# Another order for the first stage of an attention, MLP and FFN layer: step durations, hand-over gaps and leads of the planner replaced

## The chip, the cores and the metric

One Trainium2 chip, one core. The metric is the device time of one execution in microseconds (us), the median of the runs shown.

## The reference, cut to what matters

The layer works on 2 batches of 512 rows of 1024 channels. First comes a block with causal self-attention and a small gated MLP, each wrapped in a "read" and a "write" of a residual of 256 x 4 channels; then a gated feed-forward block whose three weights are a base plus a scaled sign.

```python
qkv_in = rat_read(hidden, attn_read_w, ..., 3)        # 1024 -> 3 x 256, each normalised
attn   = attention(qkv_in, qkv_w, pos)                # 16 heads of 16, rope, causal softmax
hidden = rat_write(hidden, attn, ...)                 # softplus, exp, gated update of the residual
g, u   = split(rat_read(hidden, mlp_read_w, ..., 2))
mlp    = silu(g @ ctx_w[0].T) * (u @ ctx_w[1].T)      # 256 -> 1024
hidden = rat_write(hidden, mlp, ...)
# feed-forward, 1024 -> 3584 -> 1024; each weight w of w1, w3, w2:
w      = base + mean(abs(w - base)) * sign(w - base)
out    = hidden + (silu(norm(hidden) @ w1.T) * (norm(hidden) @ w3.T)) @ w2.T
```

## The kernel before, in words

The kernel has two stages. The **second stage** is the feed-forward block: 28 slices of 128 inner channels in 14 groups of two. Products run as three fp32r passes of high and low parts: `gate` (L969, operands `xnT` and `w_hi`/`w_lo`, into PSUM) and the product with `w2` (L1068). Its order is written out by hand in each engine's loop and isn't touched.

The **first stage** is everything before it. It has 1061 steps, each a few instructions of one engine, named (stage, tile or unit, part); below I write them as `finish6.0`. The stages are:

- `front` t (8 tiles of 128 rows): layer norm, turn (L824), read product (L843), statistics, `qkv` product (L858), rope, turn into `big`.
- `fill`, `use`, `weigh`: attention in 16 groups (batch, half of the queries, quad of heads). `fill` puts scores into the four banks `quad` (L905 and L908 for the row maxima, L915 and L920 for the turned scores); `use` is the maximum on DVE (L1372) or the exponential on ACT (L1122); `weigh` is the product with the values (L878). The `quad` banks are filled one unit after another: `fill` u+1 waits for `use` u. `turnmax` turns the maxima and lowers the queries by them, `out` copies the weighed values, `row` divides by the sums.
- `back` t: the residual write after attention and the read before the MLP. `mlp` (4 blocks of 256 rows, 8 steps each): product on PE (L1022), `Silu` on ACT (L1250, into `sgate`), product on DVE (L1525, into `inner`).
- `finish` t: the write after the MLP. Part 0 is its product on PE (L952, which waits for all 8 `inner` of its block), parts 1 to 8 softplus and factors (on DVE L1416 to L1434), part 9 on POOL adds the reloaded x to `wr_q` (L1619), part 12 is SP's reload of x into `qk_xa`, parts 13 and 10 on POOL add into `hid` (L1670, L1624), part 11 on DVE are two products over 128x768 (L1438, L1441), parts 14 to 16 the statistics (last instruction L1309).
- `norm` t: scaling into `works` on ACT (L1193), turn on PE (L824), high part on ACT (L1202), low part on DVE (`xnT_lo`, L1557). `early`: the first 12 pieces of the second stage's `gate` products, for batch 0.
- `measure` n (84 weight slices): load of weight and base (SP), their difference (DVE L1547, every third on POOL L1675), sum of magnitudes on ACT (L1268). `coef` sums them up. `raw` and `prep` load the first three slices again and make weights of them: difference on POOL (L1633), sign on ACT, `coeff` times sign plus base on DVE (L1448), high part on ACT, low part on DVE (L1458).

**What sets the order.** `phase_one_order` is a list scheduler that runs when the kernel is built. Each step has an engine and a cost from `WORK` (a third number is the part for which DVE shares SBUF access with POOL), `before` lists what it depends on, and of the ready steps the one with the smallest rank is put next into its engine's program:

```python
rank = start - PULL * weight[key] - lead(key)
```

`weight` is the cost of the longest chain behind the step, for measurements `MEASURE_WEIGHT` times how many are left, and `lead` comes from the tables `FIRST` (by stage and stretch) and `AHEAD` (by part). Each engine then runs its steps strictly in this order. PSUM banks for the steps in `HOLD` and the work set of a tile are chosen in the same pass. ACT changes its table of functions when an `mlp` step follows another kind or the reverse (L1250, L1252). At the end of the stage every engine goes on with its own loop of the second stage.

## Time and profile before

| | |
|---|---|
| median of 3 runs | 1403.0 us |
| the three runs | 1399.58, 1403.0, 1406.03 us |
| profiled execution, its own time | 1408.62 us |
| its span (first to last instruction) | 1406.8 us |
| mean granted TensorE clock | 0.958 |
| busy: PE, DVE, ACT, POOL | 1292.9, 868.6, 530.1, 361.9 us |
| ACT table loads in the MLP steps (L1250, L1252) | 6 and 6 |

The profiled execution is one run. Its time lies 5.6 us above the median of the three runs, and 1.8 us above its own span. The page's strip of 40 slices (35.2 us each) has PE at 9 tenths from slice 15 on; the second stage begins at 492.65 us. Busy time of PE is no measure of its peak, since its matmuls overlap.

### The profile page before, as it was taken

What the parts mean: (1) busy time and instruction counts of PE and PEld (TensorE: products, weight loads), DVE (VectorE), ACT (ScalarE), POOL (GpSimd) and SP (SyncE); (2) the same over time, 40 slices, a digit from 0 to 9 for tenths busy, and PEclk for the clock granted to TensorE, in tenths of its full rate; (3) what the DMA queues carried; (4) which work ended last, traced back from release to release, by engine and by line L of the source; (5) the groups of instructions that cost most, each with busy time, mean ns of one, the idle gap of its engine ahead of it and who ended that gap; (6) DMA issues with size and microseconds to landing.
All of it is one profiled execution on the core that took longest, in us unless ns stands there. A gap on an engine that the chain in (4) does not pass through costs nothing.

```text
span 1406.8 us, 16747 instructions
## 1 busy us (share of the span) xinstructions
PE 1292.9 (92%) x6548; PEld 1015.8 (72%) x6548; DVE 868.6 (62%) x1135; ACT 530.1 (38%) x809; POOL 361.9 (26%) x197
## 2 busy tenths in 40 slices
PE   4887788877887899999999999999999999999998
PEld 4754555545665678888888888888788888888887
DVE  6768777778878865546564546363645546554544
ACT  4776665855655432222222222222222222222220
POOL 2222333233234422222222222222222222222210
PEclk9998988987899899999999999999999999999999
DMA  8476887577731222322222222232222232222312
GB/s 339 147 273 252 287 285 267 208 288 274 268 132 31 105 90 93 105 102 90 90 94 97 109 90 90 90 106 102 91 90 90 95 111 94 90 90 90 116 34 120
DMA packets 53826, 197.55 MB, mean 140 GB/s; under 512 B 6626, under 2 KB 6900, under 8 KB 53236
## 3 DMA queue, kind: packets, MB, share of 16 engines
q1 hardware_dynamic: 53748, 196.49, 38.7%
q8 instruction: 52, 0.85, 0.2%
q14 instruction: 26, 0.21, 0.0%
HBM read 192.27 MB, written 4.19 MB: 140 GB/s over the span
## 4 chain that ended last, share of the span: by engine, by line
PE 72%; DVE 15%; issue 5%; ACT 5%; DMA 2%; POOL 1%; SPq 0%; DVEq 0%; ACTq 0%
PE pair L969 42%; PE quad L1068 17%; PE pair L952 2%; DVE negwide L1372 2%; PE quad L915 1%; DMA ctxw<-in_mean_w 1%; DVE raw_w L1448 1%; DVE hid L1438 1%; PE pair L1022 1%; PE quad L905 1%; PE pair L843 1%; ACT prob L1122 1%; PE pair L824 1%; DVE wr_q L1425 1%; DVE big L1547 1%
## 5 line engine op out<-in xcount | busy, mean ns | idle before, releaser
L1633 POOL TENSOR_TENSOR raw_w<-raw_w,raw_base 128x1024 f32<-128x1024 f32 x84 | 215.5, 2567 | 661.5 <-DMA raw_base<-in_mean_w 661.5
L969 PE MATMUL pair<-xnT_hi,w_hi 128*128 128x512 f32 x880 | 343.8, 391 | 3.3 <-DVE xnT_lo L1557 3.3
L969 PE MATMUL pair<-xnT_lo,w_hi 128*128 128x512 f32 x880 | 343.6, 390 | 0.0
L969 PE MATMUL pair<-xnT_hi,w_lo 128*128 128x512 f32 x880 | 343.5, 390 | 0.0
L1590 DVE TENSOR_TENSOR hf<-sgf,pair 128x512 f32<-128x512 f32 x56 | 38.5, 688 | 282.1 <-PE pair L969 282.1
L1182 ACT ACTIVATE w_hi<-raw_w 128x1024 fp32r<-128x1024 f32 x84 | 88.8, 1058 | 324.0 <-DVE raw_w L1448 323.8
L969 PEld LDWEIGHTS pair<-xnT_hi,w_hi 128*128 128x128 f32 x880 | 166.1, 189 | 38.6 <-issue 2.7
L969 PEld LDWEIGHTS pair<-xnT_lo,w_hi 128*128 128x128 f32 x880 | 165.9, 189 | 34.5
L969 PEld LDWEIGHTS pair<-xnT_hi,w_lo 128*128 128x128 f32 x880 | 165.9, 189 | 34.4
L1068 PE MATMUL quad<-w_hi,h_hi 128*128 128x512 f32 x448 | 175.4, 391 | 9.3 <-DVE hid L1570 9.3
L1448 DVE SCALAR_TENSOR_TENSOR raw_w<-raw_w,coeff,raw_base 128x1024 f32<-128x1024 f32 x84 | 166.8, 1988 | 19.9 <-ACT raw_w L1165 19.9
L1068 PE MATMUL quad<-w_lo,h_hi 128*128 128x512 f32 x448 | 174.4, 389 | 0.0
L1068 PE MATMUL quad<-w_hi,h_lo 128*128 128x512 f32 x448 | 174.3, 389 | 0.0
L1570 DVE TENSOR_TENSOR hid<-hid,quad 128x512 f32<-128x512 f32 x208 | 138.1, 683 | 56.5 <-PE quad L1068 56.5
L1458 DVE TENSOR_TENSOR w_lo<-raw_w,w_hi 128x1024 fp32r<-128x1024 f32 x84 | 106.0, 1264 | 34.2 <-ACT w_hi L1182 34.2
L1286 ACT ACTIVATE h_hi<-hf 128x512 fp32r<-128x512 f32 x56 | 35.4, 632 | 230.9 <-DVE hf L1590 230.9
L1068 PEld LDWEIGHTS quad<-w_hi,h_hi 128*128 128x128 f32 x448 | 84.1, 188 | 31.0 <-issue 14.0
L1068 PEld LDWEIGHTS quad<-w_lo,h_hi 128*128 128x128 f32 x448 | 84.1, 188 | 17.7
L1068 PEld LDWEIGHTS quad<-w_hi,h_lo 128*128 128x128 f32 x448 | 84.1, 188 | 17.0
L1165 ACT ACTIVATE raw_w<-raw_w 128x1024 f32<-128x1024 f32 x84 | 87.9, 1047 | 0.0
L1281 ACT ACTIVATE sgf<-pair 128x512 f32<-128x512 f32 x54 | 32.1, 595 | 108.2 <-PE pair L969 108.1
L1595 DVE TENSOR_TENSOR h_lo<-hf,h_hi 128x512 fp32r<-128x512 f32 x56 | 51.8, 924 | 19.6 <-ACT h_hi L1286 19.6
(234 smaller groups left out, 1561.4 us busy)
## 6 DMA issues: line engine op xcount, KB each, us to landing
raw_w<-in_w SPq DMA_DIRECT2D x84, 512.0 KB, 3.8
raw_base<-in_mean_w SPq DMA_DIRECT2D x84, 512.0 KB, 4.6
part<-in_w SPq DMA_DIRECT2D x28, 512.0 KB, 4.1
part<-in_mean_w SPq DMA_DIRECT2D x28, 512.0 KB, 5.3
ctxw<-in_w SPq DMA_DIRECT2D x28, 512.0 KB, 4.8
ctxw<-in_mean_w SPq DMA_DIRECT2D x28, 512.0 KB, 6.3
big<-in_w SPq DMA_DIRECT2D x20, 512.0 KB, 3.8
big<-in_mean_w SPq DMA_DIRECT2D x20, 512.0 KB, 4.8
```

Source lines behind the costliest of these rows:

```text
L969: a = pe.matmul(banks[gate_bank(u, b)], ww[:, k, :], xx[:, k, :], start=k == 0 and n == 0, stop=k == KF - 1 and n == 2)
L1068: a = pe.matmul(banks[m % 4], hh[:, t * P:(t + 1) * P], ww[:, half * BANK:(half + 1) * BANK], start=kk == 0 and n == 0, stop=kk == GROUP - ...
L1165: act.activation(w[:, :], w[:, :], ACT.Sign).then_inc(f_sign, 1)
L1182: act.activation(hi, raws[n % RAWS][0][:, :], ACT.Copy).then_inc(f_hi, 1)
L1281: act.activation(sgf[b][:, :], banks[gate_bank(4 * g + s, b)], ACT.Silu).then_inc(g_silu, 1)
L1286: act.activation(ht[j % GROUP][0][:, b * SEQ:(b + 1) * SEQ], hf[b][:, :], ACT.Copy).then_inc(g_hhi, 1)
L1448: dve.scalar_tensor_tensor(w[:, :], w[:, :], coeff[:, k:k + 1], base[:, :], ALU.mult, ALU.add).then_inc(f_w, 1)
L1458: dve.tensor_tensor(lo, raws[n % RAWS][0][:, :], hi.bitcast(F32), ALU.subtract).then_inc(f_lo, 1)
L1570: dve.tensor_tensor(target, rows, banks[m % 4].rearrange("p (c k j) -> p c k j", c=2, j=32), ALU.add).then_inc(o_acc, 1)
L1590: dve.tensor_tensor(hf[b][:, :], sgf[b][:, :], banks[gate_bank(u, b)], ALU.mult).then_inc(g_mul, 1)
L1595: dve.tensor_tensor(ht[j % GROUP][1][:, cols], hf[b][:, :], ht[j % GROUP][0][:, cols].bitcast(F32), ALU.subtract).then_inc(g_hlo, 1)
L1633: pool.tensor_tensor(w[:, :], w[:, :], base[:, :], ALU.subtract).then_inc(f_diff, 1)
```

## The change

No instruction is added or taken out by hand, and the dependencies in `before` stay as they are. What changes are the numbers that the list scheduler works with, and two lines of its clock:

- the costs in `WORK` and `found_work`, most of them a little lower than before (exponentials, copies), the weighing and masks a little higher;
- `HOP`, the gap between a step and one that waits for it, 0.05 in place of 0.12;
- a new table `AHEAD_OF`: an engine counts as free 0.16 (PE), 0.08 (DVE), 0.09 (ACT) or 0.04 us (POOL) before its step's end;
- `MEASURE_WEIGHT`, `PULL` and all of `FIRST` and `AHEAD`.

The diff, cut to its core (line numbers of the changed kernel are 2 higher from the first stage's programs on, 3 within the scheduler):

```diff
-RAT = [("PE", 1.35), ("DVE", 0.3), ("PE", 0.25), ("ACT", 0.3), ("PE", 0.5), ("ACT", 1.7), ("DVE", 1.85, 0.2),
-       ("ACT", 0.87), ("DVE", 2.5, 0.25), ("POOL", 1.85), ("POOL", 0.75), ("DVE", 2.05, 2.05)]
+RAT = [("PE", 1.48), ("DVE", 0.27), ("PE", 0.27), ("ACT", 0.26), ("PE", 0.59), ("ACT", 1.48), ("DVE", 1.52, 0.2),
+       ("ACT", 0.83), ("DVE", 2.68, 0.25), ("POOL", 1.81), ("POOL", 0.72), ("DVE", 1.94, 1.94)]
...
-LANDING, HOP, TABLE = 2.5, 0.12, 1.3
+LANDING, HOP, TABLE = 2.5, 0.05, 1.3
+
+AHEAD_OF = {"PE": 0.16, "DVE": 0.08, "ACT": 0.09, "POOL": 0.04, "SP": 0.0}
...
-            return "PE", 0.1 + 0.53 * cols / 256
+            return "PE", 0.22 + cols / 600
...
-        free_at[engine] = start + us
+        free_at[engine] = start + us - AHEAD_OF[engine]
...
-MEASURE_WEIGHT, PULL = 4.89, 0.00247
+MEASURE_WEIGHT, PULL = 5.161, 0.00237
```

Three places where the order comes out otherwise are shown here.

**The last MLP block, DVE.** These are the steps `mlp24.2` to `mlp31.2` (`inner`), between the end of `finish5.8` and the products of the residual (`hid` with `wr_a` and `wr_q`, `finish4.11` and `finish5.11`). Before:

```order
L1525 TENSOR_TENSOR inner<-pair,sgate 128x256 x2
L1525 TENSOR_TENSOR inner<-quad,sgate 128x256
L1438 TENSOR_TENSOR hid<-hid,wr_a 128x3x8x32
L1441 TENSOR_TENSOR hid<-hid,wr_q 128x3x8x32
L1525 TENSOR_TENSOR inner<-pair,sgate 128x256
L1438 TENSOR_TENSOR hid<-hid,wr_a 128x3x8x32
L1441 TENSOR_TENSOR hid<-hid,wr_q 128x3x8x32
L1525 TENSOR_TENSOR inner<-quad,sgate 128x256
```

Now:

```order
L1527 TENSOR_TENSOR inner<-quad,sgate 128x256
L1527 TENSOR_TENSOR inner<-pair,sgate 128x256 x4
L1527 TENSOR_TENSOR inner<-quad,sgate 128x256 x3
L1440 TENSOR_TENSOR hid<-hid,wr_a 128x3x8x32
L1443 TENSOR_TENSOR hid<-hid,wr_q 128x3x8x32
```

All eight MLP products now stand ahead of the four large residual products. On POOL, the three differences of the second stage's first weights (`raw_w`) stood behind all of that tile pair's work before:

```order
L1619 TENSOR_TENSOR wr_q<-wr_q,qk_xa 128x768 x2
L1670 TENSOR_TENSOR hid<-hid,qk_xa 128x8x32
L1624 TENSOR_TENSOR hid<-hid,wr_s 128x8x32 x2
L1633 TENSOR_TENSOR raw_w<-raw_w,raw_base 128x1024 x3
```

Now they stand around `finish4.9`, right behind the last difference of a measurement (`late`):

```order
L1677 TENSOR_TENSOR late<-late 128x1024
L1635 TENSOR_TENSOR raw_w<-raw_w,raw_base 128x1024
L1621 TENSOR_TENSOR wr_q<-wr_q,qk_xa 128x768
L1635 TENSOR_TENSOR raw_w<-raw_w,raw_base 128x1024 x2
L1672 TENSOR_TENSOR hid<-hid,qk_xa 128x8x32
L1626 TENSOR_TENSOR hid<-hid,wr_s 128x8x32
L1621 TENSOR_TENSOR wr_q<-wr_q,qk_xa 128x768
```

So `finish4.13` (L1672), behind which SP reloads x for tile 5, stands behind all three of them.

**The attention's second group, PE.** `weigh1` (L878) and the scores of `fill2` (L905, L908), both ready after the first exponential. Before:

```order
L824 MATMUL pair<-ident,wideqk 128x128 x8
L858 MATMUL pair<-wqkv,yT 128x256 x6
L878 MATMUL pair<-prob,vaug 32x256 x4
L878 MATMUL pair<-prob,vaug 32x128 x4
L905 MATMUL quad<-big 128x128 x4
L908 MATMUL quad<-maskb,identb 128x128 x4
```

Now:

```order
L826 MATMUL pair<-ident,wideqk 128x128 x8
L860 MATMUL pair<-wqkv,yT 128x256 x6
L907 MATMUL quad<-big 128x128 x4
L910 MATMUL quad<-maskb,identb 128x128 x4
L907 MATMUL quad<-big 128x256 x4
L910 MATMUL quad<-maskb,identb 128x128 x4
L880 MATMUL pair<-prob,vaug 32x256 x4
L880 MATMUL pair<-prob,vaug 32x128 x4
```

The next scores stand ahead of the weighing. Over the whole stage eight `weigh` steps move behind a `fill` that stood behind them (1, 3, 5, 18, 20, 22, 29, 38) and three the other way (7, 14, 27). `fill4` had `front3.15`, `front4.13` and `weigh3` between itself and `fill3`; now `front4.11` and `front5.6` stand there.

**The first MLP block, ACT.** Before, its eight `Silu` steps (`sgate`) came in three pieces, with a table load at each end of each:

```order
L1250 ACT_TABLE_LOAD
L1250 ACTIVATE sgate<-pair 128x256
L1268 ACTIVATE big,absum<-big 128x1024
L1250 ACTIVATE sgate<-pair 128x256
L1252 ACT_TABLE_LOAD
L1152 ACTIVATE wr_a<-pair 128x256
```

Now it is one piece:

```order
L1252 ACT_TABLE_LOAD
L1252 ACTIVATE sgate<-pair 128x256 x2
L1270 ACTIVATE big,absum<-big 128x1024
L1252 ACTIVATE sgate<-pair 128x256
L1270 ACTIVATE part,absum<-part 128x1024
L1252 ACTIVATE sgate<-pair 128x256 x2
```

Four table loads less here; the third MLP block, one piece before, is in two now (`back6.18` and `finish3.7` stand between `mlp20.1` and `mlp21.1`), two loads more. The whole program has 13 table loads in place of 15. The same ordering moves the measurements back: ahead of the last exponential (`use47`) ACT had 65 of them and has 61 now, and `raw0.0` to `raw2.0` are issued by SP behind all measurements, where they stood among them before.

## Rows read from the trace of the kernel before

**Rows 1.** Windows: busy time (x instructions) of each engine, clock, DMA, by stretch

```profile
core 0: us, PE busy (x) PEld busy (x) DVE busy (x) ACT busy (x) POOL busy (x), PEclk, DMA share, GB/s
...
404.00:420.00 16.00, 14.89 (x43) 7.95 (x42) 9.98 (x28) 7.30 (x16) 4.17 (x7) 0.86 0.00 1
...
433.60:443.00 9.40, 2.49 (x23) 2.33 (x21) 9.33 (x8) 4.39 (x6) 7.14 (x3) 0.80 0.06 21
...
492.65:1406.80 914.15, 901.11 (x3960) 742.43 (x3960) 489.38 (x498) 227.15 (x274) 199.99 (x78) 1.00 0.27 95
```

**Rows 2.** Timeline of PE: start us, us, what, idle before and its releaser

```profile
442.94 2.87 PE L952 MATMUL pair<-wcat,inner 128*128 128x376 f32 x4 [6.91 <-DVE inner L1525]
```

**Rows 3.** Timeline of DVE, last MLP block

```profile
428.63 0.42 DVE L1525 TENSOR_TENSOR inner<-quad,sgate 128x256 f32<-128x256 f32 x1
...
429.56 0.42 DVE L1525 TENSOR_TENSOR inner<-pair,sgate 128x256 f32<-128x256 f32 x1 [0.30 <-ACT sgate L1250]
...
433.64 1.88 DVE L1438 TENSOR_TENSOR hid<-hid,wr_a 128x768 f32<-128x768 f32 x1
435.55 2.98 DVE L1441 TENSOR_TENSOR hid<-hid,wr_q 128x768 f32<-128x768 f32 x1
...
438.79 2.76 DVE L1438 TENSOR_TENSOR hid<-hid,wr_a 128x768 f32<-128x768 f32 x1
...
442.46 0.42 DVE L1525 TENSOR_TENSOR inner<-quad,sgate 128x256 f32<-128x256 f32 x1
```

**Rows 4.** Timeline of POOL; last its line L1633, ns min/median/max

```profile
421.97 1.82 POOL L1619 TENSOR_TENSOR wr_q<-wr_q,qk_xa 128x768 f32<-128x768 f32 x1 [6.15 <-issue]
...
432.35 8.39 POOL L1633 TENSOR_TENSOR raw_w<-raw_w,raw_base 128x1024 f32<-128x1024 f32 x3
...
L1633 POOL TENSOR_TENSOR raw_w<-raw_w,raw_base x6: 2351/2396/3055, 432.4 to 487.9; 128x1024 f32<-128x1024 f32 x6
```

**Rows 5.** Timeline of DVE: steps with two SBUF operands, and a wait for PE

```profile
424.06 0.19 DVE L1417 SCALAR_TENSOR_TENSOR wr_z<-wr_b,wr_a 128x48 f32<-128x48 f32 x1
...
449.80 0.28 DVE L1412 TENSOR_TENSOR wr_b<-pair,bias_ab 128x120 f32<-128x120 f32 x1 [1.41 <-PE pair L952]
...
462.36 1.72 DVE L1309 SCALAR_TENSOR_TENSOR x_stat<-x_stat 128x1 f32<-128x1 f32 x1
...
471.17 2.54 DVE L1438 TENSOR_TENSOR hid<-hid,wr_a 128x768 f32<-128x768 f32 x1
```

**Rows 6.** Timeline of DVE, end of the first stage

```profile
478.92 0.95 DVE L1438 TENSOR_TENSOR hid<-hid,wr_a 128x768 f32<-128x768 f32 x1
...
482.46 0.15 DVE L1305 TENSOR_SCALAR x_stat<-x_stat 128x1 f32<-128x1 f32 x1
...
483.28 2.33 DVE L1309 SCALAR_TENSOR_TENSOR x_stat<-x_stat 128x1 f32<-128x1 f32 x1 [0.60 <-POOL x_stat L1628]
...
491.37 1.23 DVE L1557 TENSOR_TENSOR xnT_lo<-quad,xnT_hi 128x1024 fp32r<-128x1024 f32 x1 [2.31 <-ACT xnT_hi L1202]
```

**Rows 7.** Timeline of ACT, first MLP block

```profile
250.38 1.28 ACT L1252 ACT_TABLE_LOAD   x1
251.67 0.38 ACT L1152 ACTIVATE wr_a<-pair 128x256 f32<-128x256 f32 x1
```

**Rows 8.** Timeline of ACT: last exponential, last measurement; then DVE's line L1547

```profile
321.07 1.45 ACT L1122 ACTIVATE prob<-quad 128x1536 f32<-128x1536 f32 x1 [2.41 <-PE quad L920]
...
403.72 1.06 ACT L1268 ACTIVATE late<-late 128x1024 f32<-128x1024 f32 x1 [0.93 <-POOL late L1675]
...
L1547 DVE TENSOR_TENSOR part<-part x28: 1207/1217/2264, 48.7 to 395.0; 128x1024 f32<-128x1024 f32 x28
```

**Rows 9.** Timelines of PE and ACT, second and third attention group

```profile
65.91 0.86 PE L878 MATMUL pair<-prob,vaug 128*32 128x256 f32 x16
...
80.63 0.50 PE L905 MATMUL quad<-big 32*128 32x128 f32 x8
...
75.48 1.45 ACT L1122 ACTIVATE prob<-quad 128x1536 f32<-128x1536 f32 x1 [0.23 <-PE quad L920]
```

More of the change, by code:

```diff
@@ L129 @@
+    "mlp": [("PE", 1.89), ("ACT", 0.38), ("DVE", 0.42)],
+    "finish": [("PE", 5.32)] + RAT[1:8] + [("DVE", 3.55, 1.25)] + RAT[9:] + [("SP", 2.0), ("POOL", 0.73), ("DVE", 1.71),
+                                                                           ("POOL", 0.55), ("DVE", 0.16, 0.16)],
+    "measure": [("SP", 3.5), ("POOL", 2.35), ("ACT", 1.25)],
     "x": [("SP", 2.0)],
     "ctx": [("SP", 7.0)],
-    "diag": [("DVE", 4.0, 4.0)],
-    "raw": [("SP", 2.0), ("POOL", 2.4), ("ACT", 1.06)],
-    "coef": [("DVE", 0.35), ("PE", 0.35), ("DVE", 0.2)],
@@ L134 @@
-    "prep": [("DVE", 1.3, 1.3), ("ACT", 1.08), ("DVE", 1.25, 1.25)],
-    "norm": [("ACT", 1.25), ("PE", 1.1), ("ACT", 1.05), ("DVE", 1.25)],
-    "early": [("PE", 1.4)] * 4,
+    "diag": [("DVE", 3.84, 3.84)],
+    "raw": [("SP", 2.0), ("POOL", 2.35), ("ACT", 1.05)],
+    "coef": [("DVE", 0.2), ("PE", 0.3), ("DVE", 0.15)],
+    "prep": [("DVE", 1.28, 1.28), ("ACT", 1.05), ("DVE", 1.22, 1.22)],
+    "norm": [("ACT", 1.24), ("PE", 1.04), ("ACT", 1.01), ("DVE", 1.21)],
+    "early": [("PE", 1.53)] * 4,
@@ new lines @@
+FIRST = {"back": (-2.4, -2.4, -2.8, -2.9), "coef": (-1.7, -2.1), "ctx": (8.5,), "diag": (32.4, 31.3), "early": (-10.5,),
+         "fill": (14.8, 1.5, -0.9, 1.2), "finish": (-0.6, -1.3, -3.7, -10.9), "front": (-4.2, -4.1, -4.5, -5.7),
+         "measure": (0.1,), "mlp": (0.8, -0.7, -0.2, -4.1), "norm": (2.8, 1.9, -3.8, -2.8),
+         "out": (-5.2, -5.7, -1.4, -5.4), "prep": (2.9,), "raw": (-3.5,), "row": (0.3, -1.1, -0.7, 2.9),
+         "turnmax": (3.2, 2.9, 1.7, 0.1), "use": (-1.6, -1.5, 8.2, -1.9), "weigh": (4.2, 1.5, 0.5, 0.4), "x": (6.1,)}
@@ new lines @@
+AHEAD = {"back": (2.8, 9.4, 8.6, 3.7, 3, 4.4, 3, 1.8, 2.1, 1.7, 5.4, 2.7, 2.2, 2.5, 0.6, 6.6, 3.6, 3, 2.7, 2, 2.6),
+         "coef": (-5.9, 3, -7.1), "ctx": (-2.3,), "diag": (-30.7,), "early": (0.4, -7.6, -2.3, -2.7), "fill": (0.1,),
+         "finish": (1.4, 3, 5.6, 3.7, 6.4, 0.6, 1.5, 0.2, 0.3, 2.7, -0.1, 2.3, 2.7, -4, -0.1, 4.4, -1.2),
+         "front": (5.2, 4.6, 5.5, 5, 14.4, 5.8, 48.1, 5.4, 5.4, 7.6, 7.5, 5.4, 4.7, 21.2, 5.8, 5.2, 5.8),
+         "measure": (3.6, 0.1, -0), "mlp": (-1.8, 0.3, 8.3), "norm": (-2.5, -11.4, 1, 9.3), "out": (5.1,),
+         "prep": (-4.3, -5.8, -8.7), "raw": (1, 0.3, -2.8), "row": (12.4, 0.9, 0.4, 4.5), "turnmax": (-0.8, 9.8),
+         "use": (2.1,), "weigh": (-1,), "x": (2.8,)}
```

38 lines of the change are left out of this document (11 added, 27 removed).

## The prediction

> **What bounds the kernel now.** I read the windows by stretch first. From 492.65 us on the second stage keeps PE busy for 901.11 of 914.15 us at full granted clock [rows 1]. Its instructions and their order stay as they are, so those 914 us stay, and the change can only move the moment at which they begin. Ahead of it no engine is full over the whole stage; what ends last changes from place to place, so I looked for the end first.
>
> PE's timeline shows the largest hole: `finish6.0` starts at 442.94 after 6.91 us idle, released by DVE's `inner` [rows 2]. DVE's timeline tells why. The eight MLP products of the last block begin at 428.63, 0.93 us apart [rows 3], but after six of them the four large products of `finish4.11` and `finish5.11` stand in the queue, mixed with the last two. And these are slow: 1.88, 2.98 and 2.76 us [rows 3], where the same instruction takes 0.95 [rows 6]. POOL's timeline shows the other side: three `raw_w` differences fill 432.35 to 440.74 [rows 4], 2.80 us each in place of the 2.40 of their median. The two engines took turns. The last `inner` ends at 442.88.
>
> From there DVE sets the pace to the end: in the windows it is busy 9.33 of 9.40 us [rows 1], and its last full statistics step ends at 482.61 [rows 6]. Then a chain of small steps follows: the final `x_stat` took 2.33 us in place of 0.15, beside the second stage's first POOL difference, and the last `xnT_lo` runs from 491.37 [rows 6]. It ends the stage.
>
> **The change, part by part.** The sum is made against the profiled execution, 1408.62 us; the median of the runs shown lies 5.6 us lower, and I shift by that at the end.
>
> (a) The last MLP block. All eight products now go first. Undisturbed, the last would end 7 x 0.93 + 0.42 = 6.9 us after the first begins, at 435.6, and `finish6.0` would start 7.3 us sooner. Against that stands POOL: `raw1.1` and `raw2.1` now follow `finish4.9`, which ended at 423.79 [rows 4], and so meet `finish5.6` and `finish5.8` on DVE. Their small products of two SBUF operands, such as the one at 424.06 [rows 5], wait while a difference runs. The nearest row is the same kind of step behind `finish6.8`, 1.72 us in place of 0.15 [rows 5, 6]; at 424.06 the wait is for a difference that has just begun, about 2.1 us, and for the next one about 0.8. Bounds: 0 (POOL early or late) and two whole differences, 4.8. I take 2.9. Then the last `inner` ends at 438.5, 4.4 us sooner.
>
> The Trainium skill, SBUF — State Buffer, section "SBUF: two separate sides", says that GpSimd and a VectorE operation with two SBUF inputs take one port pair as an exclusive lock, and that whichever starts first holds it for its whole instruction. By that rule the differences cost DVE as much beside `finish5.8` as beside `finish4.11`, which speaks against this move; the rival "lock" below is that case.
>
> DVE still has the four large products to do, 4 x 0.96 = 3.9 us, which before were done by 442.88. At 438.5 it is 4.4 us ahead in time and 3.9 us behind in work, so 0.5 is won there. Behind that, the rows show 1.41 us of waiting for `finish6.0`, 1.72 - 0.15 = 1.57 on the step at 462.36 and 2.54 - 0.95 = 1.59 on the product at 471.17 (`finish6.11` against `finish7.9`) [rows 5], 4.6 in all. I expect 2.6 to be left, since `finish6.0` ends earlier than it is needed and `finish7.8` (mostly PSUM operands) now stands between. Together DVE's last full statistics step comes 2.5 us sooner.
>
> (b) The very end. Before, 10.0 us pass from 482.61 to 492.65. In it the last turn of `norm7` waited on PE behind two `early` pieces. Now `early2.3` stands ahead of `norm7.1`, and `norm6.3` ahead of the last `x_stat`; the `early` pieces themselves begin sooner, since `norm3.3` and `prep` are through some 10 us earlier. What can't be shortened is the wait for POOL and the blocked step (0.6 + 2.33) and the last DVE step (1.23) [rows 6]; ACT, PE and ACT stand between, so I keep 8.0. Gain 2.0, between 0 and 3.5.
>
> (a) and (b) give 4.5, between 2 lost and 9 won.
>
> (c) Measurements. Four of them (61 to 64) leave the time ahead of the last exponential at 321.07 [rows 8]: three differences on DVE, 3 x 1.22 = 3.7 us [rows 8], and four magnitudes on ACT. They reappear where DVE has room: 404 to 420 is busy 9.98 of 16 us [rows 1]. Gain between 0 and 3.7; I take 3.0, as DVE is the fuller of the two.
>
> (d) Attention. In five places net (eight less three) the scores no longer wait for `weigh`, 0.86 us each [rows 9]: 4.3 at most. At one place more is moved: `fill4` began at 80.63 although its exponential had ended at 76.93 [rows 9]; two shorter steps (2.8 us) now stand there. But every other chain of the stage has to keep up, and tiles 4 to 7 of `front` are pushed back for it. Between 0 and 6; I take 2.0.
>
> (e) Tables. Four loads less in the first MLP block, 4 x 1.28 = 5.1 us of ACT [rows 7]; two more in the third block, 2.6 us, which I count at nothing, since ACT is the least busy of the three engines that hand on there (38% of the span); uncovered they would cost 2.6. In the first block ACT has gaps too, so a quarter counts: 1.3, between -2.6 and 5.1. The row shows the next activation start 0.01 us after a load's end [rows 7]. The Trainium skill, ScalarE: Activation LUTs, section "What ACT_TABLE_LOAD costs", counts about 1.38 us of drain on top, 2.66 for a switch; by that the term would be twice as large and the sum 1.4 us lower. The trace doesn't agree.
>
> The loads behind the measurements (`raw0.0` to `raw2.0`) and the later reload of x for tile 5 cost nothing as long as their cover holds: `raw2.1` ends near 429, the reload lands 4 to 5 us later, `finish5.9` is through near 436, and DVE wants it at about 444.
>
> Sum: 4.5 + 3.0 + 2.0 + 1.3 = 10.8. 1408.6 - 10.8 = 1397.8 in the profile, and **1392.2** for the median.
>
> **The rivals.**
> *Only the end moves.* (c) to (e) come to nothing, since they free an engine that others don't wait for. For it: no engine is full before 428 us, and the planner has put other work in each gap. Then -4.5, for the median 1398.5. That is no change by my measure; what a measurement of this kernel can tell from none is about 0.5%, 7 us.
> *Lock.* Every `raw_w` difference blocks one of DVE's small products for its whole 2.40 us: 3 x 2.40 = 7.2 in place of 2.9. The term (a) is gone, the rest stays: -10.8 + 4.3 = -6.5, 1396.5. It decides if POOL has its three differences ready just when `finish4.8` to `finish5.8` run.
> *The measurements come too late* (slower). After the last exponential 23 are left in place of 19. Before, the 19 took from 321 to 404.8 [rows 8], 4.4 us each; at that pace the last ends near 422. On POOL the last difference and `raw0.1`, whose load SP now issues behind all measurements, stand ahead of `finish4.9`, `finish4.13` and so of the reload for tile 5. That chain has about 8 us in hand (436 against 444), `prep0.0` more. So it decides from a last measurement at 430 on, 4.75 us each. At 5.5 it ends at 447, 17 us too late, one to one: -10.8 + 17 = +6 to +7, 1409.5. The slot that each load waits for is freed by ACT, so a slower ACT or DVE in the MLP blocks would do it.
>
> **How the numbers follow.** Forecast case 0.56, only the end 0.22, lock 0.09, too late 0.13. The forecast case's own range is 1382 to 1396 (its terms at their bounds don't all come together). The 8-in-10 range takes in the two small cases and half of the slow one: 1381 to 1405. Faster by over 0.5% (below 1396): 0.57, the forecast case and a little of the next. Within: 0.30. Slower: 0.13.
>
> **What would show it.** PE's hole in front of `finish6.0` (L954 after) shrinks from 6.9 us to under 4; the eight `inner` come in one run 0.93 apart; `finish4.11` and `finish5.11` take 0.95 to 1.0 each, and the waits turn up in L1419 and L1426. The last magnitude on ACT ends near 420 rather than 404.8. The last exponential comes 3 to 8 us sooner than 321, and the windows show 914 us from the first full batch-1 gate on, beginning near 482. It is wrong if the last exponential isn't earlier, if PE waits longer ahead of the last MLP block, or if DVE shows a wait for `coeff`. If the second stage itself changes by more than 2 us, my first sentence is wrong.

## The result, and the profile after

Beside 4 runs of the kernel before with a median of 1401.8 us, 4 runs of the changed kernel gave 1412.5 to 1428.9, median 1425.5: ratio 1.0148, 95% interval 1.0080 to 1.0217. It is slower by some 20 us; I had forecast 10.8 faster. The kernel before ran 104 times more beside the experiments, mean 1404.6 us, standard deviation 3.7; the changed one has 8 runs in all, mean 1422.6 (6.6), a loss of 18.0. Below I compare means. One execution, the profiled one of `middle_after`, took 2142.9 us at a granted clock of 0.556 and stands in no mean.

| | before | after |
|---|---|---|
| profiled execution, its span | 1408.6, 1406.8 us | 1428.9, 1427.1 us |
| mean granted clock of it | 0.958 | 0.949 |
| `fill38` begins, `use38` begins | 263.12, 269.65 | 268.42, 285.54 |
| `fill39` begins | 271.58 | 289.22 |
| last exponential, last magnitude | 321.07, 403.72 | 337.83, 439.78 |
| `finish6.0` begins | 442.94 | 460.64 |
| second stage begins, its length | 492.65, 914.15 | 511.46, 915.64 |

A step's start is that of its first instruction; `use38` is the exponential of `fill38`'s scores. The windows of the changed kernel, columns as in [rows 1] (this one was opened 0.06 us ahead of the first product), have the second stage nearly unchanged, and it begins 18.8 us later:

```profile
511.40:1427.10 915.70, 902.48 (x3960) 743.38 (x3960) 487.49 (x499) 227.17 (x275) 202.97 (x78) 1.00 0.27 95
```

Of these 18.8 us, 16.8 are there at the last exponential, and 17.6 already at `fill39`. PE's timeline of the changed kernel shows how they come about:

```profile
268.42 1.15 PE L917 MATMUL quad<-big 32*128 32x256 f32 x16 [0.20 <-DVE big L1383]
269.50 12.35 PE L1024 MATMUL pair<-inT,ctxw 128*128 128x256 f32 x56
282.78 5.32 PE L954 MATMUL pair<-wcat,inner 128*128 128x376 f32 x16 [0.93 <-DVE inner L1527]
...
289.22 0.71 PE L907 MATMUL quad<-big 32*128 32x512 f32 x3
```

At 268.42 `fill38` puts its scores into the `quad` banks. Then come the seven other products of the first MLP block (L1024) and `finish0.0` (L954, 5.32 us), and only 20.8 us later `fill39`; before, that distance was 8.5 us. ACT's timeline of the same place:

```profile
267.69 1.28 ACT L1252 ACT_TABLE_LOAD   x1
268.99 0.38 ACT L1252 ACTIVATE sgate<-pair 128x256 f32<-128x256 f32 x1
...
281.89 0.38 ACT L1252 ACTIVATE sgate<-pair 128x256 f32<-128x256 f32 x1
282.29 1.28 ACT L1254 ACT_TABLE_LOAD   x1
283.58 1.02 ACT L1233 ACTIVATE yn<-pair,stat_back 128x256 f32<-128x256 f32 x2
...
285.54 1.87 ACT L1124 ACTIVATE prob<-quad 128x2048 f32<-128x2048 f32 x1
```

The scores of `fill38` were ready at 269.57. But the exponential stands behind the whole block: eight `Silu` (L1252) that come at PE's pace, mostly 1.7 us apart, the table load back, `back2.18` and a magnitude. It begins at 285.54, 16.0 us after its scores; before, it was 5.4.

What I had looked at was right in its form. The last MLP block on DVE, to compare with [rows 3], and DVE's small steps ahead of it, with [rows 5]:

```profile
445.01 1.43 DVE L1419 SCALAR_TENSOR_TENSOR wr_z<-wr_b,wr_a 128x48 f32<-128x48 f32 x1
...
449.26 1.80 DVE L1426 TENSOR_TENSOR wr_r<-wr_r,wr_b 128x48 f32<-128x48 f32 x1
...
453.63 0.42 DVE L1527 TENSOR_TENSOR inner<-quad,sgate 128x256 f32<-128x256 f32 x1
...
460.17 0.42 DVE L1527 TENSOR_TENSOR inner<-quad,sgate 128x256 f32<-128x256 f32 x1 [0.51 <-ACT sgate L1252]
460.51 0.95 DVE L1440 TENSOR_TENSOR hid<-hid,wr_a 128x768 f32<-128x768 f32 x1
461.49 0.96 DVE L1443 TENSOR_TENSOR hid<-hid,wr_q 128x768 f32<-128x768 f32 x1
```

The eight `inner` come in one run 0.93 us apart, the large products take 0.95 and 0.96, the waits turned up in L1419 (1.43 in place of 0.19), L1424 (1.39) and L1426 (1.80), and `finish6.0` follows without a hole. The hole has gone to the front: the first `inner` comes 115.8 us after the last exponential, not 107.6. ACT's last exponential and last magnitude, which answer to [rows 8]:

```profile
337.83 1.45 ACT L1124 ACTIVATE prob<-quad 128x1536 f32<-128x1536 f32 x1 [1.61 <-PE quad L922]
...
439.78 1.04 ACT L1270 ACTIVATE late<-late 128x1024 f32<-128x1024 f32 x1
```

PE's timeline at the end of the first stage:

```profile
508.00 1.09 PE L826 MATMUL quad<-ident,work 128*128 128x128 f32 x8 [1.79 <-ACT work L1195]
511.46 0.79 PE L971 MATMUL pair<-xnT_hi,w_hi 128*128 128x512 f32 x1 [2.37 <-DVE xnT_lo L1559]
...
512.91 0.63 PE L971 MATMUL pair<-xnT_hi,w_hi 128*128 128x512 f32 x1
```

A product of that stage takes 0.79 and 0.63 us here and 0.39 later: PE had waited 1.79 and 2.37 us, and from 512 to 514 us the windows show its granted clock at 0.50, the lower of its two levels.

### The profile page after: what moved, and what is told of

It is laid out like the page before. It is cut to its first block, busy times and chain, and to the rows that moved or that the text cites. A ratio compares the mean times of both kernels' runs of the same rounds, so it can differ in the third digit from the quotient of the medians.

```text
span 1427.1 us, 16746 instructions
## 1 busy us (share of the span) xinstructions
PE 1303.3 (91%) x6548; PEld 1022.1 (72%) x6548; DVE 877.4 (61%) x1135; ACT 525.0 (37%) x807; POOL 367.9 (26%) x197
## 4 chain that ended last, share of the span: by engine, by line
PE 73%; DVE 17%; issue 5%; ACT 4%; POOL 0%; DMA 0%; SPq 0%; DVEq 0%; ACTq 0%
PE pair L971 41%; PE quad L1070 17%; DVE negwide L1374 2%; PE pair L954 2%; PE quad L917 2%; PE quad L954 2%; PE quad L907 1%; DVE raw_w L1450 1%; DVE ctxw L1549 1%; ACT prob L1124 1%; DVE wr_q L1427 1%; PE pair L860 1%; PE pair L1024 1%; DVE hid L1440 1%; DVE hid L1443 1%
## 5 line engine op out<-in xcount | busy, mean ns | idle before, releaser
L1450 DVE SCALAR_TENSOR_TENSOR raw_w<-raw_w,coeff,raw_base 128x1024 f32<-128x1024 f32 x84 | 159.9, 1905 | 21.9 <-ACT raw_w L1167 21.9
L1460 DVE TENSOR_TENSOR w_lo<-raw_w,w_hi 128x1024 fp32r<-128x1024 f32 x84 | 108.9, 1297 | 35.7 <-ACT w_hi L1184 35.7
```

What stands on the lines that cost most here:

```text
L1450: dve.scalar_tensor_tensor(w[:, :], w[:, :], coeff[:, k:k + 1], base[:, :], ALU.mult, ALU.add).then_inc(f_w, 1)
L1460: dve.tensor_tensor(lo, raws[n % RAWS][0][:, :], hi.bitcast(F32), ALU.subtract).then_inc(f_lo, 1)
```

## The experiments

Every order experiment has one edit to the planner, and above it the names of all 1061 steps in the order wanted. The short diffs further down show what moves in that list, or how it was put together:

```diff
-            rank = start - PULL * weight[key] - lead(key)
+            rank = PLACE[f"{stage}{t}.{part}"]
```

With the sequence of either kernel in it, this gives that kernel's program, whatever the costs. So the numbers of `WORK`, `HOP` and `AHEAD_OF` do nothing but set the order.

### The same kernel again, and the exponential moved ahead

`again` is the changed kernel unaltered.

> The changed kernel once more, unaltered, to see how far its own executions lie apart. Theory 'queue' (the loss comes from the order, above all from the exponential use38 that stands behind the whole first MLP block on ACT): median 1418 to 1428, and fill39 begins at 286 to 292 us in this profile too, use38 10 us or more after its scores are ready. Rival 'clock' (a lower granted TensorE clock in the run profiled made the trace look as it does): a run with a granted clock of 0.957 or more shows fill39 near 275 and a time near 1405.

Measured: mean 1422.0, ratio 1.0109 (1.0048 to 1.0171). Its profiled execution was the fastest of the four, 1414.2 us at a clock of 0.954:

```profile
252.88 1.15 PE L917 MATMUL quad<-big 32*128 32x256 f32 x16 [0.52 <-DVE big L1383]
253.95 12.35 PE L1024 MATMUL pair<-inT,ctxw 128*128 128x256 f32 x56
267.24 5.32 PE L954 MATMUL pair<-wcat,inner 128*128 128x376 f32 x16 [0.93 <-DVE inner L1527]
...
273.68 0.70 PE L907 MATMUL quad<-big 32*128 32x512 f32 x3
```

`fill38` comes at 252.88, 15.5 us sooner than in the other profile of the same program and 10.2 sooner than before; but `fill39` comes 20.8 us after it, as there. So two things must be kept apart: a fixed loss of 12 us behind `fill38`, and a stretch ahead of it whose length differs by 15 us between runs. For the same reason the last exponential of this execution, 8.4 us faster than its kernel's mean, begins at 322.24, only 1.2 us later than in the profile of the kernel before, and its second stage 2.9 us later; places are better compared within a stretch than from the start. Part of either theory holds: the time (1422.0) and the late exponential are those of "queue", but its "fill39 at 286 to 292 again" failed.

`exp_first` puts `fill38`/`use38` ahead of the first MLP step:

```diff
-PE   mlp0.0 fill38.0 mlp1.0 mlp2.0 mlp3.0 ... mlp7.0 finish0.0 finish0.2 finish0.4 fill39.0
+PE   fill38.0 mlp0.0 mlp1.0 mlp2.0 fill39.0 mlp3.0 ... mlp7.0 finish0.0 finish0.2 finish0.4
```

> One edit to the changed kernel: fill38 and use38 stand ahead of the first MLP step, fill39 and use39 behind mlp2; nothing else moves. Theory 'queue': the attention's chain gets back what it lost behind the MLP block, 8 to 12 us of the 17.6 by which fill39 was late, so the time falls to 1411 to 1417 and fill47 begins at 323 to 327 in place of 335.2. Rival 'filled anyway': the attention catches up but the first MLP block, now broken open, makes finish and the last MLP blocks late by as much; fill47 earlier by 8 us and finish6.0 (L954) by under 3, time 1421 or more. Rival 'measurements': they are what is late (60.2 by 35 us); then fill47 gains under 3 us as well.

Measured: mean 1429.2, ratio 1.0161 (1.0107 to 1.0215): nothing gained, 6.6 us above the changed kernel. Its PE:

```profile
255.39 1.22 PE L1010 MATMUL quad<-big 32*128 32x256 f32 x16 [2.26 <-DVE big L1476]
...
263.49 1.14 PE L1000 MATMUL quad<-big 32*128 32x512 f32 x8
...
272.91 3.69 PE L1117 MATMUL pair<-inT,ctxw 128*128 128x256 f32 x16 [1.32 <-DVE inner L1620]
277.54 5.32 PE L1047 MATMUL pair<-wcat,inner 128*128 128x376 f32 x16 [0.93 <-DVE inner L1620]
...
285.51 0.71 PE L1010 MATMUL quad<-big 32*128 32x256 f32 x8
```

`fill39` comes 8.1 us after `fill38`, as wanted, but `fill40` (285.51) then stands behind five more products and `finish0.0`. From `fill38` to `fill47` it takes 74.4 us in place of 66.3. The rival "filled anyway" is right in the time and in its gist, that the work is there and has to be done somewhere. Its picture was another one: it had the attention catch up and `finish` pay, but here the attention itself didn't catch up, since it waits for the same products at `fill40`.

### Where the loss arises: the two orders cut and joined

`head_before`, `head37_before` and `head24_before` take the order of the kernel before up to `weigh47`, `fill37` and `fill24`, and behind it the changed kernel's. `head24_after` is the reverse of the last. (In `head24_before` one pair more, `turnmax8.0` and `weigh24.0`, stands as in the kernel before.)

```diff
+SEQUENCE = before[:before.index("weigh47.0") + 1]
+SEQUENCE += [step for step in after if step not in SEQUENCE]
```

> The order of the kernel before up to the end of the attention (weigh47), then the order of the changed kernel. Theory: the whole loss lies ahead of that cut, and the end of the stage gains what my terms (a) and (b) say: the second stage begins 4.5 us sooner than in the kernel before, time 1395 to 1400 beside 1401.8. Rival 'shift': what stands behind the cut is worth nothing or loses (the trace of the changed kernel has its last full statistics step and its second stage 1.5 us later still than the attention's end explains): 1402 to 1405.

> The order of the kernel before up to fill37, then the changed kernel's order, which finds six MLP products already done. Theory 'deferred MLP': nothing is left of the block to stand in the way of use38; fill38 to fill47 takes 55 to 57 us in place of 66.5, and the time is 1402 to 1408, the end's 3 to 4 us of loss included. Rival 'everything behind fill38 is worse': 62 us or more from fill38 to fill47 and a time of 1411 or more.

> The order of the kernel before up to fill24, then the changed kernel's. If the changed order's own part up to fill24 prepares the low clock that follows, fill24 to fill30 takes 41 to 44 us here as in the kernel before, fill38 comes before 256, and the time is 1408 to 1414, the deferred MLP block and the end still paid. If it is the order behind fill24: fill24 to fill30 takes 46 us or more in part of the runs, and the time is 1417 to 1424.

> The changed kernel's order up to fill24, then the order of the kernel before (which first catches up on 12 measurement steps and 6 others). Theory 'deferred MLP': the loss is made between fill24 and fill47, where the changed order has the first MLP block, 8 products and 8 Silu, in one piece behind fill38: 1400 to 1406. Rival 'low clock early': the changed order's first attention groups leave TensorE at a low clock, 5 to 6 us more of it between fill24 and fill30 in two profiles; then half of the 20 us shows here too, 1409 or more.

| kernel | mean us | ratio to before, 95% | time x (1 - granted clock) | `fill38` at | `fill38` to `fill47` |
|---|---|---|---|---|---|
| before | 1404.6 | | 53.6 | 263.1 | 54.9 |
| `head_before` | 1404.9 | 0.9994 (0.9966 to 1.0022) | 52.8 | 259.1 | 54.9 |
| `head37_before` | 1412.1 | 1.0054 (1.0035 to 1.0073) | 55.9 | 260.9 | 62.9 |
| `head24_before` | 1420.5 | 1.0115 (1.0080 to 1.0150) | 67.8 | 261.6 | 67.5 |
| after (both labels) | 1422.6 | 1.0148 and 1.0109 | 69.7 | 268.4, 252.9 | 66.8, 66.3 |
| `head24_after` | 1416.2 | 1.0085 (1.0064 to 1.0105) | 60.9 | 269.6 | 53.7 |

Read downwards, each step exchanges one piece of the order: the end behind the attention 0.3 us, `fill38` to `weigh47` 7.2, `fill24` to `fill37` 8.4, all that is ahead 2.1. The sum is the 18.0 us; each difference of means is uncertain by 1 to 2.5 us. So the end, on which 4.5 of my 10.8 us rested, is worth nothing as it stands (the rival "shift"), and 15.6 of the 18.0 us lie in the attention's second half. The pieces have these prices only in this direction: `head24_after`, with the changed order up to `fill24` alone, loses 11.6 us and not 2.1. `head37_before` went with its rival (62.9, 1412); `head24_before` with its second case in the time, while `fill24` to `fill30` stayed at 43.8 in the one profile. `head24_after` lost too: it has to catch up on 18 steps left off before `fill24` and takes 53.2 us from there to `fill30` (42.8 before), so its time, which is the one that the rival named, doesn't tell its two theories apart.

What the changed order does is seen from the counts: at `fill24` it has done 12 measurement steps and 6 others fewer than the order before, at `fill38` 19 measurement steps, 17 steps of the first MLP block and 4 of `back` fewer. For that it should be ahead. No gain is seen: the eight profiles with the order before up to `fill37` and no products added have `fill38` at 257.7 to 263.1, mean 260.2; the four with the changed order at 252.9, 255.4, 266.7 and 268.4, mean 260.8. (Four profiles so far apart could hide some us.) The reason that I see, which no run isolates, is that the attention's scores wait for exponentials and these for scores, and that leaving other work off doesn't shorten that chain. The work left off is then paid for behind `fill38`: from there to `fill47` PE is busy 54.3 and 55.5 us in the two profiles of the changed kernel, and 43.6 in the kernel before.

### One step, one block: the converse in the kernel before

`finish_late` moves `finish0` and `finish1` back in the changed kernel, `finish_early` moves `finish0.0` ahead of `fill39` in the kernel before (`back4.12` and `back4.13` fall in behind `fill41` with it), `mlp_late` moves the whole first MLP block behind `fill38` there.

```diff
-PE   mlp6.0 mlp7.0 back2.19 back3.14 fill39.0 ... fill42.0 finish0.0
+PE   mlp6.0 mlp7.0 back2.19 back3.14 finish0.0 fill39.0 ... fill42.0
```

```diff
-PE   ... fill38.0 mlp6.0 mlp7.0 back2.19 back3.14 fill39.0
+PE   ... fill38.0 mlp0.0 mlp1.0 mlp2.0 mlp3.0 mlp4.0 mlp5.0 mlp6.0 mlp7.0 back2.19 back3.14 fill39.0
```

> The changed kernel with the steps of finish0 and finish1 at the progress they have in the kernel before: finish0.0 (5.3 us of PE) stands behind fill44, not ahead of fill39; all else as in the changed kernel. Theory 'finish0 holds the attention' : fill39 begins 5 to 6 us sooner after fill38 (15 in place of 20.8), fill38 to fill47 falls from 66.5 to 58 to 61, and the time by 4 to 8 us, to 1414 to 1419. Rival 'filled anyway': PE has the same products to do before fill47, the segment stays above 64 and the time within 3 us of 1422.

> The converse in the kernel before: finish0.0 alone stands ahead of fill39 (it stood behind fill42). Theory 'finish0 holds the attention': fill39 begins 4 to 6 us later after fill38 (12.5 to 14.5 in place of 8.5) and the whole of it reaches fill47 and the end, 1407 to 1410. Rival 'filled anyway': the product is saved again behind fill42, so that fill38 to fill47 stays within 2 us of 55 and the time within 2 us of 1403.5.

> The kernel before with its first MLP block (mlp0 to mlp7, products, Silu and inner) in one piece behind fill38 and ahead of use38, as the changed kernel has it; nothing else moves. Theory 'deferred MLP': the attention ahead of fill38 gets at most 3 us faster, since its scores wait for exponentials and not for PE, fill39 begins 17 to 21 us after fill38 in place of 8.5, and the time is 1410 to 1415, 6 to 10 us above the kernel before. My term (e), the rival: four table loads less, 1400 to 1404, because fill38 comes as much sooner as use38 is later.

`finish_early`: mean 1411.8, ratio 1.0044 (1.0020 to 1.0069), 7.2 us lost, all but by one step. PE of it:

```profile
260.16 1.15 PE L1010 MATMUL quad<-big 32*128 32x256 f32 x16
261.24 3.72 PE L1117 MATMUL pair<-inT,ctxw 128*128 128x256 f32 x16
...
266.96 5.27 PE L1047 MATMUL pair<-wcat,inner 128*128 128x376 f32 x16
272.17 1.14 PE L1000 MATMUL quad<-big 32*128 32x512 f32 x8
```

`fill39` comes 12.0 us after `fill38` in place of 8.5, and `fill38` to `fill47` takes 61.7 in place of 54.9. The rival is refuted; the theory holds in kind, though `fill39` comes only 3.5 us later and the rest of the 6.8 arises behind it. `mlp_late`: mean 1414.1, ratio 1.0067 (1.0042 to 1.0092), 9.5 us lost. Its PE:

```profile
255.24 1.15 PE L1010 MATMUL quad<-big 32*128 32x256 f32 x16 [0.60 <-DVE big L1476]
256.32 14.08 PE L1117 MATMUL pair<-inT,ctxw 128*128 128x256 f32 x64
...
276.13 1.24 PE L1000 MATMUL quad<-big 32*128 32x512 f32 x4 [3.57 <-ACT prob L1217]
```

and its ACT:

```profile
270.43 0.38 ACT L1345 ACTIVATE sgate<-pair 128x256 f32<-128x256 f32 x1 [1.34 <-PE pair L1117]
270.84 1.28 ACT L1347 ACT_TABLE_LOAD   x1
...
274.23 1.85 ACT L1217 ACTIVATE prob<-quad 128x2048 f32<-128x2048 f32 x1
```

The exponential waits from 256.4 to 274.23 for the block. `fill30` to `fill38` takes 43.0 us, beside 44.4 to 49.2, mean 46.6, in seven profiles with the order before, and `fill38` to `fill47` 9.4 longer. The time is the theory's. This is my term (e) by itself, four table loads less, with the opposite sign. What it doesn't separate is the two queues: the eight products stand ahead of `fill39` on PE as the eight `Silu` stand ahead of `use38` on ACT. `finish_late`: mean 1429.6, ratio 1.0181 (1.0152 to 1.0211). The segment did fall, to 63.2 us, but `fill47` to `mlp8` rose by as much (23.6 in place of 20.4), and from the last exponential to `finish6.0` it took 129.1 us (122.8 and 122.5 in the changed kernel). Neither theory has this: the mean is 7.0 us above the changed kernel, where "filled anyway" allowed 3. So undoing this one move there gains nothing.

### Measurements moved alone

`measures_before` gives the changed kernel the measurement steps, and the load of the MLP weights, at the progress (count of other steps) of the kernel before; `measures_late` the reverse.

```diff
+SEQUENCE = [each measure and ctx step where the other kernel has it, counted in other steps]
```

> The changed kernel with every measurement step and the load of the MLP weights (ctx) at the progress they have in the kernel before, all other steps in the changed kernel's order. Theory 'queue' makes no use of the measurements: under 4 us gained, 1420 to 1426. Rival 'measurements' (with term (c) wrong in sign: measurements and with them the load of the MLP weights come later, and so does the first MLP step): mlp0 begins near 250 in place of 266, and half or more of the 17 us comes back, 1408 to 1417.

> The kernel before with every measurement step and the load of the MLP weights at the progress they have in the changed kernel. My term (c): the differences and magnitudes moved out of the attention give 3 us, 1401 to 1403. Theory 'measurements carry the MLP weights': measure41, behind which that load is issued, comes later, the first MLP block stands in PE's queue and waits for it with the scores behind it; mlp0 begins 5 us or more later than 240 to 244 and the time is 1408 or more. Rival 'neither': within 2 us of 1404.6.

Means 1458.3 and 1449.2, ratios 1.0367 (1.0315 to 1.0419) and 1.0326 (1.0291 to 1.0362): some 36 and 45 us lost, both ways, and from the first attention groups on (`fill11` at 122.4 and 117.2 in place of 110.2 and 111.1). `mlp0` began at 274.8 in the first, not at 250. In `measures_late` the theory of the MLP weights is met to the letter (`mlp0` at 266.4, time over 1408), but `fill11` was late well over 100 us before that load was issued (258.51), so it isn't what these 45 us show; the other theories are off. What the two runs show is that a kind of step can't be exchanged by itself. The price of my term (c) is not measured by them, and stays open.

### The clock: cause, or company?

Over the runs of a kernel time and clock go together: of the 18.0 us between the means, 16.1 are in the column time x (1 - clock). That invites the reading that the order lowers the clock and the clock makes the loss. At one place it can be seen whole, the entry of the second stage. `early_after` puts `early2.3` ahead of `norm7.1` in the kernel before, `tail_early` moves it back in `head_before`, and `warm_entry` adds useless work to `head_before`:

```diff
-PE   norm7.1 early2.3
+PE   early2.3 norm7.1
```

```diff
                 if g == 0:
+                    readers_through(pe, [had_last[gate_bank(0, 1)]])
+                    for k in range(9):
+                        pe.matmul(banks[gate_bank(0, 1)], w13[0][0][:, k % KF, :], xnT[0][0][:, k % KF, :],
+                                  start=True, stop=True)
                     pe.wait_ge(n_lo, TILES)
```

> The converse in the kernel before: early2.3 stands ahead of norm7.1, nothing else moves. Theory 'clock at entry': PE waits 2.4 us ahead of the last gate products, the clock there shows 0.5 to 0.6, and 2 to 4 us are lost, 1404.5 to 1406.5. Rival 'same work, other place': within 1 us of the kernel before; norm7.1 is also delayed by up to 1.4 us, which is a loss without any clock, so that a time 1.4 us longer with products 0.23 apart would be the rival's too.

> The kernel head_before with one step moved: PE's early2.3 (six gate products) stands behind norm7.1 again, as in the kernel before, in place of ahead of it. Theory 'clock at entry': in head_before PE had nothing between norm7.1 (ended 485.1) and the first full batch-1 gate (487.48), its granted clock fell to 0.53, and the first 12 of these products took 0.43 us apart in place of 0.23, 2.4 us; with PE kept busy they run 0.23 apart and the time falls by 2 to 4 us, to 1399 to 1401.5. Rival 'same work, other place': the early products only move, PE waits as long ahead of norm7.1 instead, the clock falls there, and the time stays within 1 us of head_before's 1403.4.

> head_before with nine products more on PE, of no use (batch 0's xnT with the first weights, into the bank that the first batch-1 gate overwrites), ahead of PE's wait for the last xnT_lo; no step moves. Theory 'clock at entry': they fill 2.1 of the 2.4 us that PE waits, the granted clock stays at 1.00, the first 12 gate products come 0.23 us apart in place of 0.43, and a kernel with more work gets 1.5 to 2.5 us faster: 1401 to 1403 beside head_before's mean of 1404.9. Rival 'the clock falls for another reason' (the 1.8 us ahead of norm7.1, or chance): the products are still 0.43 apart, which then delays the gates by up to 1.5 us more: 1405 or more.

`early_after`: mean 1407.0, ratio 1.0017 (0.9999 to 1.0035), 2.4 us lost, which is just about the noise; in its profile the second stage is 1.7 us longer. Its windows, PEclk in the third column from the right:

```profile
486.00:488.00 2.00, 0.87 (x8) 0.63 (x6) 0.04 (x1) 1.08 (x2) 0.25 (x1) 1.00 0.00 0
488.00:490.00 2.00, 0.76 (x3) 0.67 (x4) 1.18 (x1) 1.99 (x3) 0.00 (x0) 0.95 0.00 0
490.00:492.00 2.00, 2.00 (x7) 1.52 (x6) 1.08 (x1) 0.78 (x1) 0.00 (x0) 0.50 0.00 0
492.00:494.00 2.00, 2.00 (x8) 1.58 (x7) 0.80 (x2) 0.00 (x0) 0.00 (x0) 0.70 0.00 0
```

The granted clock goes to 0.50, the level of 1.2 GHz, after PE had waited 2.37 us. `warm_entry`: mean 1402.8, ratio 0.9987 (0.9971 to 1.0003), 2.1 us less than `head_before` (1404.9), standard error 1.3, with nine products more. Its PE:

```profile
482.29 1.09 PE L919 MATMUL quad<-ident,work 128*128 128x128 f32 x8 [1.79 <-ACT work L1292]
483.14 2.34 PE L1142 MATMUL pair<-xnT_hi,w_hi 128*128 128x512 f32 x9
485.76 0.50 PE L1064 MATMUL pair<-xnT_hi,w_hi 128*128 128x512 f32 x1 [0.29 <-DVE xnT_lo L1656]
486.10 0.40 PE L1064 MATMUL pair<-xnT_hi,w_lo 128*128 128x512 f32 x1
```

and its windows:

```profile
484.00:486.00 2.00, 1.71 (x8) 1.10 (x7) 1.23 (x1) 1.97 (x3) 1.62 (x1) 1.00 0.00 0
486.00:488.00 2.00, 2.00 (x10) 1.61 (x10) 0.55 (x1) 1.31 (x2) 0.00 (x0) 1.00 0.00 0
```

The clock stays at 1.00 and the products come 0.23 us apart, where the first 12 in `head_before` came 0.43 apart: 2.4 us in the traces. Here the clock is a cause, of some 2 us; the trace shows it better than the times, which are 1.7 standard errors apart. `tail_early`: mean 1401.7, ratio 0.9984 (0.9967 to 1.0002), 3.2 us under `head_before` (standard error 1.3). In its profile PE waits 3.12 us ahead of `norm7.1` instead, and that turn and `early2.3` are at half clock; the rival named this, but the time fell as the theory had it. Why it did isn't shown.

The rest of the question went to useless transposes (`ident`, 0.13 us each at full clock) in PE's other waits:

```diff
+WARM = {step: (the bank's last user, bank, count), ...}
+                if (stage, t, part) in WARM:
+                    warm(*WARM[stage, t, part])
```

> The changed kernel with transposes of no use on PE (of ident, 0.13 us each at full clock, into a bank whose last reader is done) ahead of six steps before which it waited 1.3 to 2.6 us: fill17, turnmax6, front7.11, turnmax9, fill32, fill36; 56 of them, 7.3 us of PE. No step moves. Theory 'the clock is a cause': the granted clock stays up, less than 64 us are lost to it in place of 69.7, and the time falls to 1413 to 1419. Rival 'the clock goes along': the time stays at 1421 to 1426, the additions at best hidden in the waits; a mean of 1420 or more with an unchanged clock is that case.

> tail_early with such transposes ahead of norm5.1 (22), of norm7.1 (20) and of the wait for the last xnT_lo (11). PE waited there 3.8, 3.1 and about 1 us, and the profile of tail_early shows norm7.1 at 1.97 in place of 1.10 us and ten gate products behind it 0.43 apart. Theory: they run at full clock, the second stage's products begin 2 to 3 us sooner, 1398 to 1400 beside tail_early's mean of 1401.7. Rival 'what ends last is DVE' : the last xnT_lo (483.88) sets the entry and not PE, so at most 1 us: 1400.5 to 1402.

> warm_tail with transposes of no use ahead of nine more steps of the first stage before which PE waited 1.2 to 3.1 us (fill15, front5.15, fill21 left out, fill24, weigh24, fill35, fill47, finish2.0, early0.0). Theory 'the clock is a cause': clock loss below 46 us in place of 50, time 1393 to 1398, faster than all others. Rival 'the clock goes along' or 'fillers get in the way': 1399 to 1404, no better than warm_tail.

| kernel | mean us | ratio to before, 95% | time x (1 - clock) |
|---|---|---|---|
| after | 1422.6 | | 69.7 |
| `warm_gaps` | 1419.4 | 1.0099 (1.0066 to 1.0132) | 55.6 |
| `tail_early` | 1401.7 | 0.9984 (0.9967 to 1.0002) | 49.9 |
| `warm_tail` | 1403.4 | 0.9993 (0.9970 to 1.0015) | 50.3 |
| `warm_all` | 1400.1 | 0.9973 (0.9950 to 0.9996) | 36.9 |

Between 180 and 195 us the changed kernel had run at 0.50 throughout in its first profile and at 0.77 in the second (`again`); in `warm_gaps` it is at 1.00. The window of the changed kernel in its first profile:

```profile
180.00:195.00 15.00, 13.09 (x94) 9.00 (x90) 5.94 (x13) 6.50 (x14) 3.01 (x2) 0.50 0.55 207
```

in `again`:

```profile
180.00:195.00 15.00, 12.23 (x93) 7.66 (x93) 8.68 (x12) 8.62 (x20) 2.35 (x1) 0.77 0.46 152
```

and in `warm_gaps`:

```profile
180.00:195.00 15.00, 11.79 (x129) 8.53 (x124) 10.16 (x15) 8.81 (x19) 3.07 (x3) 1.00 0.73 262
```

14.1 us of lost clock came back, and the time fell by 3.2 (standard error 2.9), which lies between the ranges of the two theories. So a good part of the lost clock lies where PE waits anyway and costs nothing: the 14.1 us were worth hardly more than 9, and most likely 3. (What the added transposes themselves cost isn't separated.) The loss of the changed order is not the 16 us that the column seems to say. `warm_tail` brought nothing (1403.4, above both of its ranges). `warm_all`, which has fillers ahead of eight steps more, not nine, is the fastest kernel of the study, 4.5 us under the kernel before, and the only one whose interval lies wholly below it, if barely. It had 13.0 us less of lost clock than `tail_early` and was 1.6 us faster, within the noise and in the range of its rival.

`middle_after` has the changed order only between `weigh47` and `finish6.0`.

> The kernel before up to weigh47, the changed kernel's order up to finish6.0, then the kernel before to the end. Theory: the changed order is worth something only in this middle, where mlp8 to finish6 took 102.7 to 103.2 in place of 104.6 and finish6 began 2 us sooner, and its own tail gives that back (1 us to norm7.3 and 2.4 us of half clock at the entry of the second stage): 1399.5 to 1402.5, the fastest so far beside tail_early (1401.2). Rival 'shift': the tail of the kernel before waits for measurements and weights that the changed middle leaves late (last magnitude 12 us later), so coefficients and prep come late, 1404 or more.

Mean 1409.6, ratio 1.0036 (1.0017 to 1.0055): the time is that of its rival "shift". Whether for the rival's reason isn't shown, since the one profile of it is of the execution of 2142.9 us.

## Why the prediction was wrong

**The second stage.** Nearly right: 915.6 us in place of 914.2 in the first profile, but 916.8 in the second and 918.0 in `head_before`, more than the 2 us that I had named as a sign of being wrong. The first 7 to 13 products at half clock, some 0.20 us more each, are 1.4 to 2.6 us of it, which I had not thought of; the rest isn't traced.

**(a) The last MLP block, -2.5.** The picture was right (waits in L1419, L1424 and L1426; products of 0.95; no hole ahead of `finish6.0`), two sizes were off. The waits behind POOL's differences add up to 4.0 us (1.24, 1.21 and 1.59 over the undisturbed steps) where I took 2.9; the rival "lock" had 7.2. With the head of the kernel before, `finish6.0` comes 119.6, 115.5, 117.1 and 117.6 us after the last exponential in four profiles (`head_before`, `tail_early`, `warm_entry`, `warm_tail`, the same program up to there), and 120.6 to 122.3 in four with the end of the kernel before: a gain of 4 on average, as forecast (4.4), but of 2 to 6 from one profile to the next. In the changed kernel itself it is none, 122.8 and 122.5. The step that failed is the one behind it, from `finish6.0` to the end of the last full statistics step. I had 3.9 us of large products more and 2.0 of waits less, so 1.9 lost; every profile with the changed end takes 43.0 us there (`finish_late` 48.1), and the kernel before 39.7, so 3.3 are lost. Of the waits there (5.0 us, with 0.41 that I had not counted) 3.5 are left. So (a) is worth some 1 us on average, not 2.5.

**(b) The very end, -2.0.** Right in itself: 7.8 us from the last full statistics step to the second stage in place of 10.0. But it was bought by putting the last `early` piece ahead of `norm7.1`, and PE without work behind it lost about 2 at the lower clock (`warm_entry`). Nothing is left. The two terms together: 0.3 us lost by the runs, forecast -4.5. With the entry mended the means lie 2.9 (`tail_early`) and 1.8 us (`warm_entry`) under the kernel before, in intervals that just reach 1, so the sign of the two terms may well have been right.

**(c) Measurements, -3.0.** No gain is seen and the price wasn't isolated. What I overlooked stands in the planner's dependencies: the load of the MLP weights follows measurement 41. That load was issued at 251.66 and not at 224.53, and `mlp0.0` began at 266.33 and not at 243.62 (239.17 and 250.46 in `again`).

**(d) Attention, -2.0.** `fill4` came 6.4 us sooner (74.24), and by `fill8` nothing was left (97.85 beside 97.65). "Every other chain of the stage has to keep up" was the right doubt; I gave it too little.

**(e) Tables, -1.3.** This is the step that failed worst. The sign is wrong and the size a multiple: +9.5 in `mlp_late`. I priced the four loads taken out and not what stands behind a block in one piece; the sum has no term for that wait. In the trace the loads are as I took them: the next activation starts 0.01 us behind one (282.29 + 1.28, 283.58). The Trainium skill, ScalarE: Activation LUTs, section "What ACT_TABLE_LOAD costs", would have some 1.38 us more there, and again the trace doesn't agree. The order of the first MLP block lay open in the listing of the change; what I didn't ask is which step of another chain comes next on ACT. It is `use38`, and behind it the whole attention.

**What no term had.** The cuts put 15.6 us between `fill24` and `weigh47`. Two moves of that stretch cost that much in the kernel before, the block in one piece 9.5 and `finish0.0` ahead of `fill39` 7.2 (`finish_early`). The second stood in none of my terms. Whether the two add up wasn't run; and in the changed kernel, undoing either in part (`exp_first`, `finish_late`) gained nothing. So the causes are shown from the side of the kernel before; what would have to be undone together in the changed one stays open.

**The rivals.** "The measurements come too late", the slower one, had 0.13. The last magnitude came beyond 430, at 439.78, if only because all came later (the pace is 4.5 us each, not 4.75). But its mechanism can have decided little: in the first profile 16.8 of the 18.8 us stand at the last exponential, and by the cut at `weigh47` the end costs 0.3 us. Behind it the end is a little longer than elsewhere. From the last exponential to the second stage it takes 173.6 and 173.3 us in the changed kernel, 170.4 in `head_before`, with the last magnitude 101.9, 101.6 and 98.7 us after the exponential; whether these 3 us are the rival's wasn't tested. No rival of mine lay ahead of the last exponential, where nearly all the loss is by the cuts. Of my signs for a wrong forecast the first was met: the last exponential isn't earlier.

## What to carry to other kernels

When steps that save a switch are gathered into one piece, price the piece by what stands behind it on that engine: the first step there of a serial chain waits for the whole of it, and here 9.5 us were lost although ACT had 5.1 us of loads less to do. Deferring work of another chain helps a serial chain only if that work is what it waits for; look at both ends of the deferral, and take orders cut and joined at a few steps to find the place, since single kinds of steps can't be exchanged. Keep PE's last spare work for its last waits; here that was worth 2 to 3 us of 1405, in intervals that just reach 1.
